# Causal mask of the diagonal maxima: from mask products on TensorE to a copy and a fill outside it

## What is computed

```python
q = _rope(q, ROPE_THETA)
k = _rope(k, ROPE_THETA)
scores = jnp.einsum('bhqd,bhkd->bhqk', q, k) * D ** (-0.5)
causal = jnp.tril(jnp.ones((T, T), dtype=bool))
scores = jnp.where(causal[None, None], scores, -jnp.inf)
weights = jax.nn.softmax(scores, axis=-1)
out = jnp.einsum('bhqk,bhkd->bhqd', weights, v)
...
x = x + s * g
```

## Time and profile before

| | us |
|---|---|
| median of 3 runs | 738.02 (735.50 to 738.17) |
| profiled execution, time | 741.93 |
| its span, first to last instruction | 739.9 |
| TensorE busy | 639.0 |
| VectorE busy | 502.3 |
| ScalarE busy | 459.6 |
| GpSimd busy | 259.7 |
| mean granted TensorE clock | 0.935 of full speed |

### The profile page before, as it was taken

The page is one execution under the profiler, slowest core; times in us unless marked ns, Lnnn a source line. Parts: engine busy times, 40 slices in busy tenths (PEclk is TensorE's granted clock), DMA queues, the critical chain, the costliest instruction groups (busy, mean ns, idle before and its releaser), DMA issues.

```text
span 739.9 us, 14157 instructions
## 1 busy us (share of the span) xinstructions
PE 639.0 (86%) x5052; PEld 296.8 (40%) x5052; DVE 502.3 (68%) x825; ACT 459.6 (62%) x909; POOL 259.7 (35%) x459
## 2 busy tenths in 40 slices
PE   1587389899997998999989994999999999999965
PEld 0355032234534764433325442452333333356622
DVE  7965568677774643786866673888998898944212
ACT  1453046476574568778747773677677776755781
POOL 4655020232331001667402123692131221108781
PEclk9788569899998999999999996999999999999996
DMA  5057321402025301222613044053331320300001
GB/s 168 2 175 155 109 76 57 88 31 65 30 66 143 115 1 50 46 61 91 167 43 84 12 140 85 9 151 120 91 70 39 81 65 2 66 1 2 2 15 43
DMA packets 33323, 52.09 MB, mean 70 GB/s; under 512 B 5832, under 2 KB 23912, under 8 KB 30696
## 3 DMA queue, kind: packets, MB, share of 16 engines
q1 hardware_dynamic: 31960, 50.74, 25.8%
q10 hardware_dynamic: 1296, 0.46, 0.3%
HBM read 37.29 MB, written 13.63 MB: 69 GB/s over the span
## 4 chain that ended last, share of the span: by engine, by line
PE 64%; DVE 10%; ACT 6%; DMA 6%; issue 6%; POOL 5%; SPq 2%; POOLq 0%; ACTq 0%; DVEq 0%
PE ps L1317 59%; DVE maxes L1300 3%; DMA qop<-shiftH 3%; ACT probs L1032 3%; SPq L734 2%; PE ps L1532 1%; DMA F<-in_w 1%; DVE sine L1154 1%; POOL F L899 1%; PE ps L1409 1%; ACT L1032 1%; PE ps L1371 1%; DMA qop<-shiftT 1%; POOL probs L860 1%; POOL gate L548 1%
## 5 line engine op out<-in xcount | busy, mean ns | idle before, releaser
L1300 DVE TENSOR_REDUCE maxes<-ps 128x2 f32<-128x1024 f32 (+2 forms) x288 | 339.3, 1219 | 106.1 <-PE ps L1317 104.2
L1032 ACT ACTIVATE probs<-ps 128x512 f32<-128x512 f32 x576 | 306.3, 605 | 128.6 <-PE ps L1317 126.9
L1317 PE MATMUL ps<-qop,kop 128*128 128x512 bf16 (+3 forms) x768 | 186.0, 340 | 33.0 <-DMA qop<-shiftH 20.2
L860 POOL TENSOR_SCALAR_AFFINE_SELECT probs<-probs 128x512 f32<-128x512 f32 (+1 forms) x160 | 83.7, 547 | 244.5 <-ACT probs L1032 244.3
L1317 PE MATMUL ps<-probs,vals 128*9 128x512 f32 (+3 forms) x1536 | 152.9, 498 | 7.7 <-POOL probs L860 6.5
L1317 PE MATMUL ps<-kmx,qmx 32*128 32x128 bf16 (+2 forms) x1280 | 102.7, 270 | 14.7 <-DVE maxes L1300 7.1
L1317 PEld LDWEIGHTS ps<-qop,kop 128*128 128x128 bf16 x768 | 61.1, 100 | 131.2 <-ACT probs L1032 63.1
L1317 PEld LDWEIGHTS ps<-kmx,qmx 32*128 32x128 bf16 x1280 | 38.7, 94 | 117.9 <-issue 78.6
L1317 PE MATMUL ps<-F 128*128 128x128 f32 (+2 forms) x640 | 78.1, 285 | 5.3 <-DMA F<-in_w 4.2
L1317 PEld LDWEIGHTS ps<-F 128*128 128x128 f32 (+2 forms) x640 | 70.1, 183 | 21.2 <-issue 15.6
L1317 PEld LDWEIGHTS ps<-probs,vals 128*9 128x9 f32 x1536 | 29.1, 90 | 65.3 <-issue 49.9
(11 more groups left out here) (158 smaller groups left out, 636.9 us busy)
## 6 DMA issues: line engine op xcount, KB each, us to landing
qop<-q_thirds SPq DMA_DIRECT2D x48, 192.0 KB
kop<-k_thirds SPq DMA_DIRECT2D x48, 192.0 KB
qmx<-q_thirds SPq DMA_DIRECT2D x16, 256.0 KB
kmx<-k_thirds SPq DMA_DIRECT2D x16, 256.0 KB
F<-in_w SPq DMA_DIRECT2D x16, 256.0 KB, 4.9
q_thirds<-third SPq DMA_DIRECT2D x8, 384.0 KB, 3.3
k_thirds<-third SPq DMA_DIRECT2D x8, 384.0 KB, 3.4
q_thirds<-third SPq DMA_DIRECT2D x8, 256.0 KB, 2.6
```

The lines of the kernel that those rows point to most:

```text
L860: last = pool.affine_select(where, where, [[0, number], [1, P]], ALU.is_ge, 0.0, base=0, channel_multiplier=-1)
L1032: act.activation(probs[:, u % RING, :], bank(at), ACT.Exp, scale=SCALE).then_inc(s_cells_read, 1)
L1300: dve.tensor_reduce(dst, src, AX.X, ALU.max).then_inc(s_units_read[pair // 2], 1)
L1317: return pe.matmul(out_, lhsT, rhs, start=first, stop=last)
```

## The change

- The diagonal patterns leave `PATTERN`; `max` has 7 patterns and 14 units a group. Four `dmax` units a group make the diagonal scores, unmasked. `maskq` and its products are gone.
- ScalarE copies the two banks of a `dmax` unit to SBUF (`dia`, two places) and thereby frees the pair; GpSimd fills the part above the diagonal with -1e30 in place by affine_select; VectorE reduces from SBUF (`diag_top`). `top` waits for these maxima as well.
- `shiftH` has one place instead of two: ScalarE copies the second part only after the first part's DMA has landed.
- The planner knows the new steps; `STAY` becomes a table by the present tiling (26 whole, 104 rows, 20 columns, 10 halves); all offsets in `MORE` are new, so the order of all engines changes.
- F, a shared work area, is 256 floats a partition smaller.

```diff
-PATTERN = [[(2, 0, 256), (3, 0, 256)], [(1, 0, 128), (3, 256, 128), (5, 512, 128), (7, 768, 128)],
-           [(i, P * i, 128) for i in range(4)]] + [[(i, 0, 512)] for i in (4, 5, 6, 7)] + [
-    [(6, 512, 256), (7, 512, 256)], [(i, P * i, 128) for i in range(4, 8)]]
-NM, DIAGONAL = 2 * len(PATTERN), (2, 8)
+PATTERN = [[(2, 0, 256), (3, 0, 256)], [(1, 0, 128), (3, 256, 128), (5, 512, 128), (7, 768, 128)]] + [
+    [(i, 0, 512)] for i in (4, 5, 6, 7)] + [[(6, 512, 256), (7, 512, 256)]]
+DIAGONAL = [[(i, P * i, 128) for i in range(first, first + 4)] for first in (0, 4)]
+NM, ND = 2 * len(PATTERN), 2 * len(DIAGONAL)
...
-UNITS_DONE = {0: 6, 1: NM, 2: NM}
+UNITS_DONE = {0: (4, 2), 1: (NM, ND), 2: (NM, ND)}
...
-SHAPE, STAY = {"max": "rows", "pv": "columns", "eo": "halves"}, 10.0
+SHAPE = {"max": "rows", "dmax": "rows", "pv": "columns", "eo": "halves"}
+STAY = {"whole": 26.0, "rows": 104.0, "columns": 20.0, "halves": 10.0, None: 0.0}
...
-LATER = {"lt": "soft", "lg": "comb"}
+LATER = {"lt": "soft", "lg": "comb", "dmax": "copy"}
...
+    "max": (COLUMN * BANK, "D", (("DVE", 1.2),)), "dmax": (COLUMN * BANK, "D", ()), "copy": (0, "", (("ACT", 1.1),)),
+    "fill": (0, "", (("POOL", 1.25),)), "diag_top": (0, "", (("DVE", 1.15),)),
...
+    if kind == "dmax":
+        return [("ldmax", n)]
+    if kind == "copy":
+        return [("dmax", n, u)] + ([("diag_top",) + divmod(ND * n + u - 2, ND)] if n or u >= 2 else [])
+    if kind == "fill":
+        return [("copy", n, u)]
+    if kind == "diag_top":
+        return [("fill", n, u)] + ([("top", n - 1, parts(n - 1)[-1])] if n and u == 0 else [])
...
+        dia = sb("dia", [P, 2, 2 * BANK])
...
-        shiftH = sb("shiftH", [2 * HG, 2, BANK], BF16)
+        shiftH = sb("shiftH", [2 * HG, BANK], BF16)
...
+                elif kind == "fill":
+                    n, u = arg
+                    copied = UNIT["dmax", n, u]
+                    pool.wait_ge(s_units_read[copied % 2], copied // 2 + 1)
+
+                    where = dia[:, u % 2, :].rearrange("p (n c) -> p n c", c=P)
+                    pool.affine_select(where, where, [[0, 8], [-1, P]], ALU.is_ge, NEG, base=0, channel_multiplier=1
+                                       ).then_inc(s_filled, 1)
...
+                elif kind == "copy":
+                    n, u = arg
+                    filled = UNIT["dmax", n, u]
+                    pair = 2 * (filled % 2)
+                    act.wait_ge(s_units_full, filled + 1)
+                    wait(act, s_diagonal, ND * n + u - 1)
+                    act.activation(dia[:, u % 2, :], two_banks(pair).rearrange("p n c -> p (n c)"), ACT.Copy
+                                   ).then_inc(s_units_read[pair // 2], 1)
...
-                        act.activation(shiftH[:, part, :], bank(at)[0:2 * HG, 0:BANK // 2].bitcast(BF16), ACT.Copy
+                        if part:
+                            act.wait_ge(s_shift_in[0][n % 2], 16 * (n // 2 + 1))
+                        act.activation(shiftH[:, :], bank(at)[0:2 * HG, 0:BANK // 2].bitcast(BF16), ACT.Copy
...
+                elif kind == "diag_top":
+                    n, u = arg
+                    half, heads = u // 2, 2 * (u % 2)
+                    dve.wait_ge(s_filled, ND * n + u + 1)
+                    if u == 0 and n:
+                        dve.wait_ge(s_rowtop, NTH["top", n - 1, parts(n - 1)[-1]])
+                    dve.tensor_reduce(maxes[:, heads:heads + 2, 4 * half:4 * half + 4, 3],
+                                      dia[:, u % 2, :].rearrange("p (h n c) -> p h n c", h=2, n=4), AX.X, ALU.max
+                                      ).then_inc(s_diagonal, 1)
...
-                    pe.wait_ge(s_masks, 32)
-                    if diagonal:
-                        for k in range(2):
-                            mm(bank(pair + k).rearrange("p (n c) -> p n c", n=4), identb[:, :],
-                               maskq[:, :].unsqueeze(1).to_broadcast([P, 4, P]), True, False)
```

More of the change, by code:

```diff
@@ L126 @@
 HOP, TILING, COLUMN, COLUMN4, LAND, FIRST = 0.2, 0.1, 0.000425, 0.0017, 4.0, 3.0
-SHAPE, STAY = {"max": "rows", "pv": "columns", "eo": "halves"}, 10.0
+SHAPE = {"max": "rows", "dmax": "rows", "pv": "columns", "eo": "halves"}
+STAY = {"whole": 26.0, "rows": 104.0, "columns": 20.0, "halves": 10.0, None: 0.0}
 WINDOW, KEEP, REGAIN = 3.4133, 0.48, 0.8
-WEIGHT = {"max": 0.25, "shift": 0.25}
+WEIGHT = {"max": 0.25, "dmax": 0.25, "shift": 0.25}
 ENGINES = ("PE", "ACT", "DVE", "POOL", "SP")
 MORE = {
[L135 to L142, removed]
@@ new lines @@
+    "add": (39, 65), "attT": (-7, -76), "colsum": 8, "comb": 36, "count": -4, "ct": 2, "diag": -72, "diag_top": -1,
+    "disp": 32, "emb": -21, "embT": 58, "embstat": -74, "eo": 83, "es": -52, "exp": (0, 1), "fill": -40, "halve": (37, 31),
+    "heads": (-56, 108), "hid": -10, "hid1": -11, "high": (-71, 54), "ldexp": (65, -47), "ldf1": -74, "ldmax": (-5, 25),
+    "ldw": -10, "ldwA": 33, "ldwB": 45, "left": (-74, -67), "lg": -3, "limit": 25, "ln": -80, "lnroot": 69, "lnstat": -3,
+    "logit": -21, "low": (-27, 44), "lt": -13, "mask": (11, -40), "max": (1, 10), "middle": (-51, -28), "mix": 1,
@@ L143 @@
+    "norm": (106, 62), "offs": 11, "out": (0, 99), "proj": (-31, -5), "pv": (-10, 1), "pvout": (-64, -40), "qk": (-12, 23),
+    "rT": -31, "rden": (120, -70), "res": 15, "root": (-6, 100), "routes": -14, "rs": -58, "shift": (0, 28),
+    "silu": (56, 20), "slot": 2, "soft": -8, "stat": (-43, 67), "store": (33, -80), "sum": (-2, 119), "top": (39, -50),
+    "total": 3, "v": (-69, 16), "wg": 19, "xT": (-56, -6), "xr": 23, "xrT": 93, "z": 4,
 }
 OF_GROUPS = ("max", "exp", "pv", "top", "shift", "halve", "pvout", "out", "mask", "ldmax", "ldexp")
-LATER = {"lt": "soft", "lg": "comb"}
+LATER = {"lt": "soft", "lg": "comb", "dmax": "copy"}
@@ L300, in needs @@
         return [("store", n // NG, 2 * (n // GB % 2) + 1), ("store", n // NG, 2 * (n // GB % 2))] + (
-            [("max", n - 2, NM - 1)] if n >= 2 else [])
+            [("max", n - 2, NM - 1), ("dmax", n - 2, ND - 1)] if n >= 2 else [])
     if kind == "ldexp":
@@ L305, in needs @@
         return [("ldmax", n)] + ([("top", n - 1, parts(n - 1)[-1])] if n and u == 0 else [])
+    if kind == "dmax":
[6 more added lines that the diff above has]
+        return [("fill", n, u)] + ([("top", n - 1, parts(n - 1)[-1])] if n and u == 0 else [])
     if kind == "top":
-        return [("max", n, UNITS_DONE[c] - 1)] + (of_part("halve", n - 2, c) if n >= 2 else [])
+        units, diagonal = UNITS_DONE[c]
+        return [("max", n, units - 1), ("diag_top", n, diagonal - 1)] + (of_part("halve", n - 2, c) if n >= 2 else [])
     if kind == "halve":
@@ L383, in streams @@
     made.append([("max", n, u) for n in groups for u in range(NM)])
+    made += [[(kind, n, u) for n in groups for u in range(ND)] for kind in ("dmax", "copy", "fill", "diag_top")]
     made += [[(kind, n, part) for n in groups for part in parts(n)] for kind in ("top", "halve", "shift")]
@@ L482, in schedule @@
         fed = [r for r in now if price[r[1]][0]]
-        alike = lambda r: STAY if SHAPE.get(r[1][0], "whole") == tiling else 0.0
+        alike = lambda r: STAY[tiling] if SHAPE.get(r[1][0], "whole") == tiling else 0.0
         if idle:
@@ L1290, in _ @@
                     dst = maxes[:, heads:heads + 2]
-                    if pattern in (0, 7):
+                    if pattern in (0, 6):
                         i = 2 if pattern == 0 else 6
                         src, dst = both.rearrange("p h (n c) -> p h n c", n=2), dst[:, :, i:i + 2, 1]
-                    elif pattern == 1 or pattern in DIAGONAL:
-                        i = 4 * DIAGONAL.index(pattern) if pattern != 1 else 0
-                        src = both.rearrange("p h (n c) -> p h n c", n=4)
-                        dst = dst[:, :, 1:TB:2, 2] if pattern == 1 else dst[:, :, i:i + 4, 3]
+                    elif pattern == 1:
+                        src, dst = both.rearrange("p h (n c) -> p h n c", n=4), dst[:, :, 1:TB:2, 2]
                     else:
-                        src, dst = both, dst[:, :, 1 + pattern, 0]
+                        src, dst = both, dst[:, :, 2 + pattern, 0]
                     dve.tensor_reduce(dst, src, AX.X, ALU.max).then_inc(s_units_read[pair // 2], 1)
+                elif kind == "diag_top":
[7 more added lines that the diff above has]
+                                      ).then_inc(s_diagonal, 1)
                 elif kind == "top":
                     n, part = arg
-                    done = UNITS_DONE[part]
-                    for u in (done - 2, done - 1):
+                    units, diagonal = UNITS_DONE[part]
+                    for u in (units - 2, units - 1):
                         last = UNIT["max", n, u]
                         dve.wait_ge(s_units_read[last % 2], last // 2 + 1)
+                    dve.wait_ge(s_diagonal, ND * n + diagonal)
                     if n >= 2:
@@ L1484, in _ @@
                             rows_h = slice(MR * h, MR * h + MR)
```

(4 more changed lines are left out.)

21 lines of the change are left out of this document (8 added, 13 removed).

## The result

The changed kernel took 756.6 us (median of 4 runs, 753.2 to 761.1) beside 738.1 of the kernel before: a ratio of 1.026, 95% interval 1.020 to 1.031. It is 18.5 us slower; 713 was forecast.

A forecast was written before the change was run, and what follows sets the result against it. TensorE was taken as the bound, with VectorE nearly full in the second layer. Masks 24.3 us plus merging 3 less shift buffer 2 gave 25.3 us, so 713 from 738.0; forecast range 701 to 726, 8-in-10 range 697 to 735.

The forecast's parts named there:

- Prices of the new steps: Diagonal units: ScalarE copy 1.11 us, GpSimd fill 1.10 us, VectorE reduction from SBUF 1.22 us, 64 of each.
- All 64 are 34.6 us ... How much comes through: Mask products on TensorE: 0.54 us for each of 64 diagonal units, 34.6 us, of which 24.3 would be gained.
- The occupancy limit of 0.92: Four long attention stages: a second engine beside TensorE may reach 0.92 busy; with ScalarE's copies added, 18.2 us come through.
- Groups are one ahead of their exponentials, so this is covered: Diagonal unit's chain grows some 2.2 us and two hand-overs; claimed hidden except in groups 0 and 8.
- rival 1: ScalarE's copies delay exponentials and hold TensorE 0.27 us a copy, 17 us; gain about 10, time 728; chance 0.17.
- rival 2: Second and fourth stage: in-order queues pass the copy on to TensorE; slower, 751 to 774 us; chance 0.10.
- The order. One thing can be priced: Re-planned queues: neighbouring diagonal units' score products may merge on TensorE, 10.6 us if all 32 pairs do; 3 taken.
- A sign that the prediction had named for being wrong: Wrong on the high side if TensorE's waits for ScalarE or GpSimd sum to over 20 us.
- The single shift buffer: Group 8: ScalarE's second shift copy must wait for the first half's DMA; 2 us charged, between 0 and 6.
- Rival 3: More than forecast: all 34.6 us of masks and 10.6 of merging come, 693 us; chance 0.10 for under 701.
- Rival 4: Shared port: GpSimd's fills stop VectorE's routing operations in the fourth stage, 4 us, result 717; chance 0.03.
- The low end of the range: 701 us: adds 7.6 us of merging and half of 10.3 us of TensorE's time given to ScalarE and waits.

The follow-up runs named there:

- run 1: Kernel before without its mask products, every queue in the same order, causal mask left out of the maxima: 722.7 us, ratio 0.981.
- run 4: Changed kernel in its own order, but ScalarE's copy of a diagonal unit moves 8 of 1024 elements, every wait kept: 753.2 us, ratio 1.022.
- run 6: Changed kernel's order without copy, fill and SBUF reduction; VectorE reduces the unmasked diagonal units from PSUM: 754.1 us, ratio 1.022.
- run 13: All new steps in the order of the kernel before (run 9), but without GpSimd's fill; VectorE waits for ScalarE's copy alone: 761.5 us, ratio 1.030.
- run 18: Kernel before without mask products (run 1), with one place for the shift rows instead of two: 722.4 us, ratio 0.978.
- run 17: New steps without fills in the order of the kernel before (run 13), with ScalarE's copy moving 8 of 1024 elements: 754.4 us, ratio 1.021.
- run 5: Changed kernel in its own order, but GpSimd's fill covers one of the eight blocks of a unit, every wait kept: 751.4 us, ratio 1.017.
- run 3: Changed kernel's steps planned with the old offsets and a bonus of 10 for every tiling: 785.7 us, ratio 1.066.
- run 9: All new steps in the order planned for the kernel before; copy and fill right behind each diagonal unit, reduction two units later or before top: 782.8 us.
- run 10: As run 9, but the diagonal units take the 1st, 2nd, 7th and 8th place of each group: 803.5 us, ratio 1.088.
- run 15: As run 9, but each fill stands behind the next unit of maxima in GpSimd's queue: 778.3 us, ratio 1.053.
- run 8: Changed kernel in its own order with four bf16 places in dia instead of two of f32: 756.1 us, ratio 1.024.

## Why the prediction was wrong

Put together, by the steps that a run does and the order in which it does them:

| us | old order | new order |
|---|---|---|
| with mask products | 738 | 767 |
| without them, no chain | 723 | 754 |
| chain without fill, copy of 8 elements | 754 | |
| chain without fill | 761 | |
| chain, GpSimd's work but no hand-over | 766 | |
| whole chain | 783 | 757 |

The forecast put chain and order together at 3 us of gain, less 2 for the shift buffer. They cost 33 us (723 to 757). How that splits depends on which comes first. By the new order without a chain it is 31 for the order and 2 for the chain. By the chain in the old order it is 60 for the chain, of which the new order saves 26. Either way 738 - 15 + 33 gives the 757, within 1 us.

- **Prices of the new steps: right.** 1.05, 1.10 and 1.21 us against 1.11, 1.10 and 1.22. Two rows of one line were enough for the fill. The Trainium skill ("VectorE: DVE Perf Modes", TRN2 errata) would have the SBUF reduction some 65 ns shorter (an estimate from that page). By these rows it is 7 ns shorter than the 1221 that the PSUM form took in the same profile, so the trace doesn't agree, and it was right to go by the rows. ScalarE's busy time went to 508 us and not to 530: its 64 copies have 66.7 us of records, but there are five table loads of 1.28 us fewer, and the rest is not explained.
- **"All 64 are 34.6 us ... How much comes through": mis-sized.** I let 24.3 us through; the mask products were worth 14.6 in the old order and 12.5 in the new. The occupancy limit of 0.92 was aimed at ScalarE, which has no copies in run 1. Of the 34.6 us only 25.5 left TensorE's busy time. Some 5 of the missing 9 are the clock: TensorE was busy 73 us at the lower level in run 1 beside 63 before (an estimate from these two numbers); the other 4 are not explained. And 9 of the 25.5 came back as idle time, the largest part in waits for VectorE's reduction of maxima (7.5 to 14.1 us). Here a step taken from an engine at 0.97 gave back only what the next one in the ring of two bank pairs left over.
- **"Groups are one ahead of their exponentials, so this is covered": the step that failed.** The chain of copy, fill and reduction was costed by its engine time and by the border between layers. Its price is the hand-over: in the order of the kernel before it costs 60 us, of which 12 are ScalarE's and GpSimd's work (7 and 5) and 48 the passing on through queues, slower matmuls with it. The forecast took nothing for it; rival 1 took a quarter of a copy's time as passed on, from one absence of ScalarE, and rival 2, at two thirds and more, had a chance of 0.10. In the changed order the chain alone costs 2 us, but that order costs 31 itself.
- **"The order. One thing can be priced": failed as well.** I counted 3 us for merged pairs and nothing for the rest. More merged than I counted: by their weight loads, blocks of maxima in TensorE's stream went from 241 to 226 when the masks left (run 1), 5 us by the 0.33 us of the earlier trace rows, and to 198 in the changed kernel, 9 us more. No such further gain is seen: TensorE was busy 613.5 us in run 1 and 614.6 in run 4, which has the changed order and a record of every matmul. A sign that the prediction had named for being wrong did come: TensorE's waits for ScalarE and GpSimd sum to 68 us (27 before), and over 20 was the mark; with 27 there before the change it was a weak sign. The order itself costs 31 us with the same steps. The chain costs 2 us in it, which run 6 and the changed kernel can't tell from nothing. In the sum of the change: -14.6 for the masks, +31 for the order, +2 for the chain, 18.5.
- **The single shift buffer: charged 2 us, nothing measured.** ScalarE stood 6.6 us once in run 13, as foreseen, but the time shows none of it: 722.4 in run 18 beside 722.7 in run 1.
- **Rivals.** Rival 2 had the sign and named the queues, and its 751 is near, but its mechanism, a copy's length passed on to TensorE, is not what runs 4 and 17 show; that it was near is luck. Rival 1, ScalarE as the limit, is refuted (3 us for all of its copying, 7 in the old order). Rival 3 didn't come. Rival 4 is real and small: beside a fill of 515.96 to 517.18 us a VectorE operation took 1.00 us that takes 227 ns in the kernel before, and VectorE's busy time grew by 5.7 us in all (by 2.0 with the fills of run 5, an eighth as large, and by 0.3 without any in run 6). The low end of the range, by the terms given for it, adds up to 700 and not 701.

```profile
515.96 1.22 POOL L882 TENSOR_SCALAR_AFFINE_SELECT dia<-dia 128x1024 f32<-128x1024 f32 x1 [1.25 <-ACT dia L1060]
...
516.26 1.00 DVE L1136 TENSOR_SCALAR F<-F 128x128 f32<-128x128 f32 x1
```

What stays open: why the order made for the chain runs 31 us longer than the old one. Of its parts only this is known: the new bonus table alone costs 42 us on the old steps, and the loss sits in layer 1. An order that carries the chain and keeps 723 was not found; runs 3, 9, 10 and 15 carry it in four other orders, and all were slower than the changed kernel.

A version that beats both kernels is run 1, or run 18 with less memory (0.981 and 0.978 of the kernel before): no mask in the maxima at all. Softmax divides out whatever is subtracted from a row, so the maximum of a row may run over keys that the mask later removes, as long as it isn't so much larger that the exponentials vanish; on these inputs it isn't.

## What to carry to other kernels

When a step leaves the fullest engine and comes back as a chain over others, count the hand-overs, not the busy time: each link sits in an in-order queue, and here three links of about 1 us each, on 64 units, cost 60 us in an order not made for them, in queues that were two fifths to two thirds busy. Where a planner lays the order, a change has two prices, the steps in the old order and the order with the old steps; both can be measured, and neither could be read off the waits of the final trace, which named the link that happened to be last. The two prices need not add: here they are 60 and 31, and both together 33. And before a mask is made cheaper, ask whether the quantity needs it at all.

## What the hardware showed unexpectedly

A ScalarE copy of 128x1024 from PSUM took 1045 ns on average (997 at best), less than the exponential of that shape, which also sums its row (1120 in the same profile). GpSimd's fill took 1091 ns in the middle of run 9's 64 and up to 1332. A bf16 `dia` changed neither: in run 8 the medians are 1032, 1091 and 1211 ns for copy, fill and reduction, against 1024, 1091 and 1211 in f32 (run 9).
